# Query projections of seven tiles: the rounded part subtracted by TensorE in PSUM, the result written by ScalarE, the third projection a slot sooner

## The reference

```
x = x + _L0_xattn_ref(_layernorm(x), ctx_2048, ...)   # banded attention over 256 positions, 8 heads of 8
x = x + _L0_ffn_ref(_layernorm(x), ...)               # top half of the rows through 256 -> 1024 -> 256, gelu
x = x + _L1_xattn_ref(_layernorm(x), ctx_2048, ...)   # 32 query heads, 8 key heads
x = x + _L1_ffn_ref(_layernorm(x), ...)               # relu squared, experts, layer norm

# in _L0_xattn_ref
qkv = transpose(mask, (0, 2, 1)) @ w_in.T + b_in
scores = einsum('bqhd,bkhd->bhqk', q, k) / sqrt(8);  band = |i - j| <= 64
attn = softmax(where(band, scores, neg));  o = attn @ v
out = (relu(o @ w_out.T + b_out) * encodings) @ w_ct + b_ct
```

## Time and profile before

| | |
|---|---|
| median of 3 runs | 342.35 us (341.98 to 342.72) |
| profiled execution | 340.92 us, span 339.2 us |
| granted TensorE clock | 0.998 of full speed |
| PE busy | 307.2 us, 91% of the span |
| PE weight load | 239.0 us, 70% |
| DVE busy | 236.2 us, 70% |
| ACT busy | 199.6 us, 59% |
| POOL busy | 181.8 us, 54% |

### The profile page before, as it was taken

The page is one execution under the profiler, slowest core; times in us unless marked ns, Lnnn a source line. Parts: engine busy times, 40 slices in busy tenths (PEclk is TensorE's granted clock), DMA queues, the critical chain, the costliest instruction groups (busy, mean ns, idle before and its releaser), DMA issues.

```text
span 339.2 us, 7193 instructions
## 1 busy us (share of the span) xinstructions
PE 307.2 (91%) x2166; PEld 239.0 (70%) x2166; DVE 236.2 (70%) x921; ACT 199.6 (59%) x414; POOL 181.8 (54%) x294
## 2 busy tenths in 40 slices
PE   1987999999999999999898998869899999999993
PEld 1966667777676767776587886647567677988892
DVE  6777788999999998984526346665788746661264
ACT  3757987878787888777640334376778953113210
POOL 5667565676785946585712712453342822335643
PEclk9999999999999999999999999999999999999999
DMA  7999010101010110100000000000000000000000
GB/s 188 366 371 332 3 44 7 46 3 41 12 33 15 25 25 19 32 2 4 2 0 0 0 2 0 0 2 1 2 1 2 0 2 0 3 31 15 18 31 31
DMA packets 13301, 14.51 MB, mean 43 GB/s; under 512 B 2512, under 2 KB 11984, under 8 KB 13264
## 3 DMA queue, kind: packets, MB, share of 16 engines
q1 hardware_dynamic: 12688, 13.72, 13.0%
q10 hardware_dynamic: 576, 0.33, 0.3%
HBM read 10.64 MB, written 1.05 MB: 34 GB/s over the span
## 4 chain that ended last, share of the span: by engine, by line
PE 61%; DVE 17%; issue 8%; ACT 6%; POOL 5%; DMA 1%; SPq 0%; POOLq 0%; DVEq 0%; ACTq 0%
PE S L752 6%; PE S L418 6%; PE O L445 5%; PE ST L429 4%; DVE masked L1251 4%; PE ST L777 4%; PE S L554 4%; PE S L628 2%; PE S L695 2%; PE PJ L672 2%; PE O L709 2%; PE XB L527 2%; PE PJ L383 2%; PE PJ L393 2%; PE XB L684 2%
## 5 line engine op out<-in xcount | busy, mean ns | idle before, releaser
L1251 DVE CUSTOM_DVE_ANT_0 masked<-S,band 128x192 bf16<-128x192 f32 x256 | 80.3, 353 | 14.1 <-PE S L418 13.0
L870 ACT ACTIVATE ex<-ST 128x384 f32<-128x384 f32 x128 | 61.4, 489 | 14.6 <-PE ST L429 12.6
L1055 POOL TENSOR_SCALAR rstd<-mv 128x1 f32<-128x1 f32 x40 | 12.0, 301 | 79.9 <-DVE mv L1206 79.8
L418 PE MATMUL S<-qk 128*128 128x384 f32 x128 | 53.4, 417 | 0.1
L429 PE MATMUL ST<-qk 128*128 128x192 f32 x256 | 47.7, 269 | 2.2 <-ACT ex L870 1.9
L429 PEld LDWEIGHTS ST<-qk 128*128 128x128 f32 x256 | 45.0, 189 | 4.5 <-issue 3.5
L1113 POOL TENSOR_SCALAR_AFFINE_SELECT ex<-ex 128x512 f32<-128x512 f32 x32 | 21.3, 665 | 30.3 <-ACT ex L870 30.1
L418 PEld LDWEIGHTS S<-qk 128*128 128x128 f32 x128 | 24.1, 188 | 17.3 <-issue 15.3
L445 PE MATMUL O<-ex,v 128*32 128x192 f32 x512 | 34.1, 338 | 0.0
L1393 DVE TENSOR_REDUCE mw<-S 128x8 f32<-128x512 f32 x32 | 21.9, 686 | 13.0 <-PE S L628 13.0
L840 ACT ACTIVATE hs<-PJ,sb,byhead 128x512 fp32r<-128x512 f32 x29 | 22.6, 779 | 12.5 <-PE PJ L384 12.0
(11 more groups left out here) (200 smaller groups left out, 709.2 us busy)
## 6 DMA issues: line engine op xcount, KB each, us to landing
qk<-kp SPq DMA_DIRECT2D x48, 48.0 KB
w<-in_w SPq DMA_DIRECT2D x2, 1024.0 KB, 10.0
cx<-in_cx SPq DMA_DIRECT2D x1, 1024.0 KB, 9.2
up<-in_up SPq DMA_DIRECT2D x1, 1024.0 KB, 11.6
down<-in_down SPq DMA_DIRECT2D x1, 1024.0 KB, 11.6
out<-x SPq DMA_DIRECT2D x8, 128.0 KB, 1.7
cxT<-in_cxT SPq DMA_DIRECT2D x1, 768.0 KB, 6.7
x<-in_x SPq DMA_DIRECT2D x1, 768.0 KB, 8.5
```

The costliest lines, as they stand in the source:

```text
L418: mm(out, r32(qp[:, t % 2, g, b, P * c:P * c + P]), r32(mv_), start=True, stop=True).then_inc(s["pe_s"], 1)
L870: A(ex[:, (n // 2) % 4, 2 * w:2 * w + 2, :], ST[n % 2][:, 0:2 * WIN].rearrange("p (h k) -> p h k", h=2), ACT.Exp, scale=SCALE).then_inc(s[ ...
L1251: last = V.tensor_tensor_reduce(out=masked[:, n % 2, h, :], in0=S[n % 2][:, WIN * h:WIN * h + WIN], in1=band[:, c, :], scale=1.0, scalar=N ...
```

## The change

For tiles 1 to 7 and the queries (n = 2, 3) the DVE instruction of line 1343 goes. In its place PE issues one more matmul into PJ, with a new constant tile `minus` (minus the identity) as weights and hs as the moving operand, on top of the projection's sum; ACT then writes PJ + bias into qp. So that the sum can go on, the start flag now stands only at the first matmul of a projection. Projection 2 moves from slot 11 to slot 10 (PROJ_LATER), its hs from slot 12 to 11. The subtractions stand in slots 11 and 14 on PE (SUB), the writes in slots 12 and 15 on ACT (SUBBED). Every wait for dve_mix of a query becomes a wait for act_sub or pe_sub.

```
+        minus = sb("minus", [P, P])
+        PROJ_LATER = {3: 0, 7: 1, 10: 2, 13: 3}
+        SUB = {11: 2, 14: 3}
+        SUBBED = {12: 2, 15: 3}
...
+        def mixed(t, i):
+            if t == 0:
+                return s["dve_mix"], i + 1
+            return (s["dve_mix"], 2 * t + 3 + i) if i < 2 else (s["act_sub"], 2 * t - 3 + i)
...
                 if t >= 1:
-                    pe.wait_ge(s["dve_mix"], 4 * t + n)
+                    pe.wait_ge(*(mixed(t, n - 1) if n else mixed(t - 1, 3)))
...
+            def subtract(t, n):
+                if (t, n) == (1, 2):
+                    pe.wait_ge(s["act_minus"], 1)
+                pe.wait_ge(s["act_hs"], 4 * t + n + 1)
+                mm(PJ[:, :], r32(minus[:, :]), r32(hs[:, n % 2, :]), start=False, stop=True, skip_group_check=True).then_inc(s["pe_sub"], 1)
...
+                    if T_ >= 0 and l in SUB:
+                        subtract(T_ + 1, SUB[l])
+                    if l in proj_slots(T_ + 1):
+                        project(T_ + 1, order(T_ + 1)[proj_slots(T_ + 1)[l]])
...
+                    if T_ >= 0 and l in SUBBED:
+                        n = SUBBED[l]
+                        act.wait_ge(s["pe_sub"], 2 * t - 3 + n)
+                        if t >= 2:
+                            act.wait_ge(s["pe_st"], UNITS * (t - 2) + 8 + 4 * (n % 2) + 4)
+                        A(r32(qp[:, t % 2, n % 2, :, :].rearrange("p b q -> p (b q)")), PJ[:, :], ACT.Identity, bias=b0[:, n:n + 1])\
+                            .then_inc(s["act_sub"], 1)
...
+                    A(r32(minus[:, :]), ident[:, :], ACT.Copy, scale=-1.0).then_inc(s["act_minus"], 1)
...
-                if l in MIX and 0 <= t < TILES:
+                if l in MIX and 0 <= t < TILES and (t == 0 or MIX[l] < 2):
```

More of the change, by code:

```diff
@@ L155, in build @@
                  "act_hs act_v act_mt act_exp act_o act_bt act_relu act_xh act_sb "
-                 "dve_w dve_band dve_ln dve_xn dve_xl dve_mix dve_max dve_rc dve_on dve_x dve_zero "
+                 "dve_w dve_band dve_ln dve_xn dve_xl dve_mix pe_sub act_sub act_minus dve_max dve_rc dve_on dve_x dve_zero "
                  "pool_var pool_rstd pool_mw pool_y pool_xn pool_fxn pool_kb pool_sel pool_zero act_kb ld_kb0 ld_kb1 dve_spread dve_masks dve_v1 ld_sel "
@@ L168, in place, with proj_slots, subtracted @@
             return T_ + off, r
+        def proj_slots(t):
+            return PROJ if t == 0 else PROJ_LATER
+        def mixed(t, i):
+            if t == 0:
+                return s["dve_mix"], i + 1
+            return (s["dve_mix"], 2 * t + 3 + i) if i < 2 else (s["act_sub"], 2 * t - 3 + i)
+        def subtracted(t, i):
+            return mixed(t, i) if t == 0 or i < 2 else (s["pe_sub"], 2 * t - 3 + i)
         def live(tile, r):
@@ L349, in _ @@
             for t in range(2, TILES):
-                sp.wait_ge(s["dve_mix"], 4 * t + 2)
+                sp.wait_ge(*mixed(t, 1))
                 for b in range(2):
@@ L382, in project @@
                 for b in range(2):
-                    mm(bank[:, T * b:T * b + T], r32(w0h[:, n, :]), r32(xs[:, b, :]), start=True, stop=False)
-                    last = mm(bank[:, T * b:T * b + T], r32(w0l[:, b, n, :]), r32(xs[:, b, :]), start=False, stop=True)
+                    mm(bank[:, T * b:T * b + T], r32(w0h[:, n, :]), r32(xs[:, b, :]), start=(b == 0), stop=False, skip_group_check=True)
+                    last = mm(bank[:, T * b:T * b + T], r32(w0l[:, b, n, :]), r32(xs[:, b, :]), start=False, stop=True, skip_group_check=True)
                 last.then_inc(s["pe_proj"], 1)
+            def subtract(t, n):
[3 more added lines that the diff above has]
+                mm(PJ[:, :], r32(minus[:, :]), r32(hs[:, n % 2, :]), start=False, stop=True, skip_group_check=True).then_inc(s["pe_sub"], 1)
             def values(t):
-                pe.wait_ge(s["dve_mix"], min(4 * t + 5, 4 * TILES))
+                pe.wait_ge(*(mixed(t + 1, 0) if t + 1 < TILES else mixed(t, 3)))
                 if t == 0:
@@ L412, in slot_ @@
                     if r in (0, 4):
-                        pe.wait_ge(s["dve_mix"], 4 * t + 3 + g if t else 2 + 2 * g)
+                        pe.wait_ge(*(mixed(t, 2 + g) if t else mixed(0, 1 + 2 * g)))
                     if n >= 2:
@@ L491, in slot_ @@
                 if T_ + 1 >= 0 and T_ + 1 < TILES:
-                    if l in PROJ:
-                        project(T_ + 1, order(T_ + 1)[PROJ[l]])
+                    if T_ >= 0 and l in SUB:
+                        subtract(T_ + 1, SUB[l])
+                    if l in proj_slots(T_ + 1):
+                        project(T_ + 1, order(T_ + 1)[proj_slots(T_ + 1)[l]])
                 if l == 5 and 0 <= T_ < TILES:
@@ L831, in slot_ @@
                 if 0 <= t < TILES:
-                    if l - 1 in PROJ:
-                        n = order(t)[PROJ[l - 1]]
-                        m = 4 * t + PROJ[l - 1]
+                    if T_ >= 0 and l in SUBBED:
[5 more added lines that the diff above has]
+                            .then_inc(s["act_sub"], 1)
+                    if l - 1 in proj_slots(t):
+                        n = order(t)[proj_slots(t)[l - 1]]
+                        m = 4 * t + proj_slots(t)[l - 1]
                         act.wait_ge(s["pe_proj"], m + 1)
@@ L838, in slot_ @@
                         if m >= 2:
-                            act.wait_ge(s["dve_mix"], m - 1)
+                            act.wait_ge(*subtracted((m - 2) // 4, (m - 2) % 4))
                         A(r32(hs[:, m % 2, :]), proj_bank(t, n)[:, :], ACT.Identity, bias=sb0[:, n:n + 1], scale=part0[:, n // 2:n // 2 + 1])\
@@ L1339, in slot_ @@
                         dve.wait_ge(s["ld_kb1"], KB_DMA * (t - 2))
-                    if n >= 2 and t >= 2:
-                        dve.wait_ge(s["pe_st"], UNITS * (t - 2) + 8 + 4 * g + 4)
                     dst = (qp[:, t % 2, g, :, :] if n >= 2 else kp[:, g, :, :]).rearrange("p b q -> p (b q)")
```

## The result

| | before | after |
|---|---|---|
| median beside each other on one chip | 342.17 us (341.34 to 342.72, 4 runs) | 349.42 us (348.28 to 350.69, 4 runs) |
| profiled execution | 340.92 us | 349.11 us |
| granted clock | 0.998 | 0.995 |

The ratio is 1.021 (95% interval 1.019 to 1.023): 7.2 us slower. The prediction said slower by 3.2 us and 345.5 us; the direction is right, the size is less than half of what came, and 349.42 lies above the range, whose upper end was 347.9.

What follows compares the result with a forecast made beforehand. PE (17.22 of 18.03 us) and DVE (16.89) nearly full, neither alone the bound. Tiles 2 to 5 2.0, tile 6 0.5, tile 1 0.4, tile 0 0.3: together 3.2 us, forecast 345.5 us, range 341.9 to 347.9.

Steps and rivals of the forecast that it cites:

- Removed, first DVE instruction: DVE's 748 ns instructions in slots 12 and 15 go; the first lies in the chain, the second does not hold what follows.
- Added on PE: 14 matmuls of 512 columns, 0.24 us each, and 0.25 more for a restart after a wait.
- Added on ACT: 14 writes of 128x512 from PSUM, 0.7 us of queue time each, 9.8 us in seven tiles.
- Moved projection: Projection 2 goes ahead of the scores of slot 11: the same four matmuls, only those scores come 0.48 us later.
- The walk: Slots 11 to 0: PE waits 0.38 for hs, slot 12's scores +0.88, slot 15 +0.49, period 18.5; chance 0.60.
- Tile 0, 1 and 6: Terms for the tiles outside 2 to 5: 0.3, 0.4 and 0.5 us slower.
- from 122.89 the chain is DVE's: Slots 0 to 4, up to the next key part: no slack and nothing lost, so that part comes about 0.49 us later.
- the check of ACT behind it: ACT's queue up to slot 3: transposed scores +0.9 there, +0.4 to +0.6 at projection 0, not on top.
- ACT becomes the bound: Rival: late exps and copy of O in slots 15 to 2 hold PE, 0.9 a tile, 348.6 us; chance 0.13.
- The gain: Rival: DVE is the bound and PE subtracts without idling, -0.24 a period, 340.7 us; chance 0.17.
- It cancels: Rival: wait 0.38 and restart stay, but DVE and POOL come early enough to give back all, 342.3 us; chance 0.10.
- What the profile after would show: Signs: PE idle 0.4 before each tile's first subtraction, period 18.4 to 18.6, DVE down 10.5 us, L460 without a wait.

Runs made afterwards that it cites:

- e_only3: Only query part 3 done the new way, part 2 left with DVE and projection 2 in slot 11 as in the kernel before; 345.68 us.
- e_later: The changed kernel with each subtraction a slot later (slots 12 and 15) and its write too (13 and 0 of the next tile); period 18.87 us.
- e_move: The kernel before with only projection 2 a slot sooner (slot 10) and no subtraction on PE; ratio 0.9988, period 18.03 us.
- e_fix: The changed kernel with one wait more: GpSimd's second select in slot 0 waits for both DVE subtractions into xs; 345.98 us, period 18.65.
- n_after: The changed kernel with GpSimd's triangular selects shrunk to one column, so the band's corners are not cleared; period 18.65 us.
- e_later_fix: The changed kernel with both subtractions a slot later and GpSimd's select held until the subtractions into xs are done; 343.70 us, period 18.28.
- d_act: The kernel before with one idle 128x512 ACT instruction added in slot 15 of tiles 0 to 6; medians differ by 4.4 us.

## Where the prediction was right and where it failed

- *Removed, first DVE instruction, in the chain; second, not.* The rows of before bear this out, and no run contradicts it; none takes either away alone. e_only3 shows that part 3 as a whole moves the period by 0.0 once the collision is taken off.
- *Added on PE, 0.24 each and 0.25 for a restart.* Right: 0.50 in the chain where it waited, 0.29 behind the four matmuls of L518 (e_later), 0.43 behind products with the values. In slot 14 it was priced at 0.43 and took 0.50: hs ended at about the same moment, PE had a wait of 0.03, and it paid the restart all the same.
- *Added on ACT, 0.7 of queue time.* Right in size (687 ns median). What it does behind it was wrong, see below.
- *Moved projection: nothing by itself.* Right: e_move.
- *The walk.* Its first wait came as said, PE idle for 0.39 until hs is done (said 0.38). The PE row names DVE as the releaser, but L410 waits for act_hs alone, and the row of its weight load names hs:

```profile
122.65 0.78 ACT L874 ACTIVATE hs<-PJ,sb,byhead 128x512 fp32r<-128x512 f32 x1
...
123.48 0.19 PEld L410 LDWEIGHTS PJ<-hs,minus 128*128 128x128 f32 x1 [0.58 <-ACT hs L874]
123.48 0.50 PE L410 MATMUL PJ<-hs,minus 128*128 128x512 f32 x1 [0.39 <-DVE mw L1286]
```

  The scores of slot 12 ended at 124.16. That is 8.69 after the key part, 7.80 before: +0.89, said +0.88. Slot 15: L460 (L485) without a wait, as said; its end came +0.63 later, said +0.49, of which the restart in slot 14 is 0.07. e_fix puts the walk at +0.62 for a period of its own.
- *Tile 0, 1 and 6.* Said +0.3, +0.4, +0.5. Without the collision (n_after) they came as -0.05, +0.40, +0.61, and the sum over seven tiles as +3.5, said +3.2.
- ***The step that failed*** is "from 122.89 the chain is DVE's, which holds no slack and has lost nothing there", and with it the check of ACT behind it. I followed the late exps to PE, found that PE just does not wait for them, and stopped. They also release GpSimd's selects. GpSimd stood in my steps only as the engine that L475 waits for; its selects were in none of them, and DVE's durations depend on what GpSimd does beside them. In the trace of before the two subtractions stood as 0.42, and I took a duration for a constant. It was one there by 0.05 us in one case and by the order of start in the other. In its place the runs show +0.65 a tile in five tiles, 3.3 us: with it the prediction's own sum comes to 345.5 + 3.3 = 348.8, against 349.42. That the first part of the sum (3.2 said, 3.5 measured) agrees so well is in part luck: tile 0 was said +0.3 and came as -0.05, against a walk that came 0.13 a tile longer in tiles 2 to 5.
- *The rival "ACT becomes the bound"* named the cause, late exps behind the write in slot 15, and came to 348.6. But its mechanism is not what happened. It needed PE to wait for exps, and in after the exps cost PE 0.7 us in the whole run, less than the 1.9 of before, and no product with the values waited for the copy of O:

```profile
PE ST L454 <- ACT ex L904: 0.7, 2, 0.5
```

e_fix settles it: with ACT's queue as it is in after, and only the select held back, the second cost is gone. A time near the right one from a mechanism that did not act is no confirmation of it.
- *The gain* was excluded by the wait in slot 11, as argued, and in e_later_fix it did not come without that wait either: 18.28, not 17.79. As far as these traces show, DVE's relief is worth only what PE idles for DVE in slots 12 to 15, and the second subtraction stands behind that stretch, where PE's own work is the chain.
- *It cancels* did not hold either.
- *What the profile after would show.* The wait ahead of the first subtraction (0.39), little ahead of the second (0.03) and L460 (L485) without a wait came. A period of 18.4 to 18.6 (19.31) and DVE down by 10.5 (4.8) did not. Nor were the transposed scores of slot 3 held by L910, the successor of L876: they began 0.28 behind the scores ahead of them in both kernels (131.54 behind 131.26, 124.30 behind 124.02).

Left open: a kernel with the first subtraction in slot 12, the second in slot 14 and the select held back was not run. Each of the two is swallowed where the other is away, but both would draw on the same wait of PE, so whether they are free together is not known.

## What to carry to other kernels

When a change adds work to a queue, follow the instructions behind it to all engines that they release, the idle ones too, and ask beside what those will now run; here VectorE's subtractions of two SBUF inputs and GpSimd's selects took turns, and the one that started second paid. Before taking a duration from a trace as given, look at its smallest and largest value and at what ran beside it: here a margin of 0.05 us held it up. If the collision falls on the engine that sets the end, a wait on the engine with slack can be worth more than it costs: the wait of e_fix gave back 0.66 us in each of five tiles.

## What the runs showed of the hardware

- A VectorE subtraction of 64x256 with both inputs in SBUF took 0.42 alone. Where a 128x512 affine select on GpSimd had begun 0.10 to 0.23 before it (all forty places in the timelines of after, e_later, e_only3 and d_act), it took 0.68 to 0.81 and ended 0.27 or 0.28 after the select. Where the select was within 0.05 of its end (before), it took 0.42. With VectorE first by about 0.1, the select took 0.81 or 0.82 in place of 0.64.
- In the chain of after a matmul of 512 columns takes 0.50 behind a gap of 0.03, as much as behind the wait of 0.39 in slot 11; in the chain of e_later, with no wait, it took 0.43 behind products with the values and 0.29 behind the matmuls of L518. Between 0.03 and 0.39 the length of the wait made no difference.
- An instruction on ScalarE that nobody reads, 0.72 us in a queue with gaps, made the period of a tile 0.60 us longer and the kernel 1.4% slower (d_act).
